# The values of a windowed cross attention: from 64x64 tiles in halves to 32x64 tiles by blocks of 32 keys

## What is computed

```python
qh, kh = rope(q @ wq.T), rope(k @ wk.T)             # 16 heads of 64
vh = v @ wv.T
scores = einsum('bhqd,bhkd->bhqk', qh, kh) * 64 ** -0.5
window_mask = (j <= i) & (j >= i - 32)              # i: query, j: key
probs = softmax(where(window_mask, scores, -1e30))
out = einsum('bhqk,bhkd->bhqd', probs, vh)          # then out @ wo.T
```

## Time and profile before

| what | value |
|---|---|
| device time, median of 3 runs | 756.9 us (753.03 to 758.53) |
| span of the profiled execution | 754.4 us |
| other time given for the profiled execution | none |
| mean granted clock of TensorE | 0.972 |
| TensorE busy (matmuls) | 712.6 us, 94% |
| VectorE / ScalarE / GpSimd busy | 540.6 / 533.2 / 530.1 us |

### The profile page before, as it was taken

One profiled execution on the slowest core, in us unless ns is written; L12 is line 12 of the kernel. 1 busy time (PEld: TensorE's weight loads), 2 busy tenths in 40 slices (PEclk: granted clock), 3 DMA queues, 4 the chain that ended last, 5 costly groups with the idle time before them and its releaser, 6 DMA issues. The chain is left out here.

```text
span 754.4 us, 31316 instructions
## 1 busy us (share of the span) xinstructions
PE 712.6 (94%) x11673; PEld 592.2 (79%) x11673; DVE 540.6 (72%) x1406; ACT 533.2 (71%) x1943; POOL 530.1 (70%) x875
## 2 busy tenths in 40 slices
PE   6889999999999999999999999999999998699990
PEld 4577788888888888888888888888888887577560
DVE  2466777777777777777787888778777776457660
ACT  2267777877777777888887877777778777555550
POOL 3266676777777877888777777777777777456554
PEclk7799999999999999999999999999999999899995
DMA  6000000211111000000000000000000000241420
GB/s 239 4 18 9 10 10 13 69 38 38 38 39 38 17 18 26 24 25 24 25 25 24 24 25 25 25 24 25 25 32 10 11 10 10 58 127 55 128 63 16
DMA packets 22802, 27.61 MB, mean 37 GB/s; under 512 B 3448, under 2 KB 18684, under 8 KB 22656
## 3 DMA queue, kind: packets, MB, share of 16 engines
q1 hardware_dynamic: 19152, 17.80, 7.8%
q0 software_dynamic: 2784, 6.56, 2.4%
q10 hardware_dynamic: 720, 1.26, 0.5%
HBM read 16.82 MB, written 9.24 MB: 35 GB/s over the span
## 5 line engine op out<-in xcount | busy, mean ns | idle before, releaser
L1123 ACT ACTIVATE PX<-P,mx 128x128 f32<-128x128 f32 x512 | 186.0, 415 | 10.1 <-DVE mx L704 10.1
L1406 POOL TENSOR_TENSOR PX<-PX,mx 128x512 f32<-128x512 f32 x128 | 130.6, 1040 | 13.5 <-DVE mx L709 13.3
L1123 ACT ACTIVATION_READ_ACCUMULATOR PX<-P,mx 128x1 f32 x512 | 130.6, 255 | 0.0
L643 DVE TENSOR_REDUCE nmf<-P 128x4 f32<-128x512 f32 x128 | 79.4, 682 | 17.5 <-PE P L226 17.5
L704 DVE TENSOR_REDUCE mx<-P 128x4 f32<-128x512 f32 x128 | 82.9, 669 | 2.6 <-PE P L326 2.6
L1132 ACT ACTIVATE PT<-P 128x512 f32<-128x512 f32 x128 | 69.7, 599 | 20.3 <-PE P L339 20.3
L1401 POOL TENSOR_TENSOR rq<-rq,tq 128x1024 f32<-128x1024 f32 x32 | 75.8, 2369 | 2.9 <-DVE tq L668 2.9
L1396 POOL TENSOR_TENSOR rk<-rk,tk 128x1024 f32<-128x1024 f32 x32 | 75.9, 2372 | 0.0
L1366 POOL CAST nm<-nmf 128x16 bf16<-128x16 f32 x32 | 6.4, 199 | 98.0 <-DVE nmf L643 98.0
L291 PE MATMUL P<-wvT,cxT 128*128 128x512 f32 x128 | 70.8, 635 | 0.4 <-ACT nmT L1080 0.4
L1087 ACT ACTIVATE PS<-P 128x512 f32<-128x512 f32 x128 | 66.5, 614 | 3.8 <-PE P L247 3.7
(11 more groups left out here) (179 smaller groups left out, 1831.4 us busy)
## 6 DMA issues: line engine op xcount, KB each, us to landing
ew<-in_ew SPq DMA_DIRECT2D x9, 384.0 KB, 3.7
xrow<-z_xs SPq DMA_DIRECT2D x24, 136.0 KB, 2.1
z_xs<-c SPq DMA_DIRECT2D x16, 136.0 KB, 3.0
x<-in_x SPq DMA_DIRECT2D x32, 64.0 KB, 2.0
cxT<-in_ctxT SPq DMA_DIRECT2D x31, 64.0 KB, 1.8
wk<-z_xs SPq DMA_DIRECT2D x6, 136.0 KB, 2.1
wvT<-z_xs SPq DMA_DIRECT2D x6, 136.0 KB, 2.1
tab<-in_tab SPq DMA_DIRECT2D x1, 512.0 KB, 7.5
```

Of the source, the lines that this page charges most:

```text
L643: dve.tensor_reduce(nmf[b % 2][:, 0, r, :], v3(bank(f"s{r}")), AX.X, ALU.max, negate=True).then_inc(S["v_bm"][r], 1)
L1123: t = act.activation(PX[(4 * b + r) % 6][:, c, :], p[:, c * 128:c * 128 + 128], ACT.Exp, bias=m[:, 0, r, c:c + 1], scale=1.0, accum_out=m[ ...
L1406: pool.tensor_tensor(X[:, :, :], X[:, :, :], mx[b % 3][:, 2, r, :].rearrange("p (h a) -> p h a", a=1).to_broadcast([128, 4, 128]), ALU.mul ...
```

## The change

The values are computed per block of 32 keys: for each head four matmuls, block r (32 rows of V, 32 of PT) with the 64 queries that see it (32 for r = 3), each block into a bank of its own (pv0 to pv3), the even and the odd head in the two halves of the output's partitions. That is eight 32x64 tiles. All 16 heads of a batch stay in the four banks, and one signal `t_pv` comes at the end of both halves. pv0 and pv2 together cover every query once, pv1 and pv3 the queries that see a second block. ScalarE copies pv2 and pv0 (512 columns each) into oX, VectorE adds pv3 (256 columns) and pv1 (512 columns) onto it. The banks are 2, 4, 5 and 6 in place of 5, 0, 2 and 4; the waits of `c_v`, `d_pt` and `d_wo` follow the merged signals. The calls of `d_pv(b, 0)` and `d_pv(b, 1)` in the written order become one `d_pv(b)` in the same place.

```diff
-            def d_pv(b, k):
-                lo = take(f"lo{k}", b, (S["s_ox"][k], b + 1))
-                hi = take(f"hi{k}", b, (S["v_ox"][k], b + 1))
-                pe.wait_ge(S[f"s_v{k}"], b + 1)
-                for u in range(2):
-                    pe.wait_ge(S["s_pt"][2 * k + u], b + 1)
-                for q in range(4):
+            def d_pv(b):
+                p = [take("pv0", b, (S["s_ox"], 2 * b + 2)), take("pv1", b, (S["v_ox"], 2 * b + 2)),
+                     take("pv2", b, (S["s_ox"], 2 * b + 1)), take("pv3", b, (S["v_ox"], 2 * b + 1))]
+                for k in range(2):
+                    pe.wait_ge(S[f"s_v{k}"], b + 1)
                     for u in range(2):
-                        pe.matmul(lo[64 * u:64 * u + 64, 96 * q:96 * q + 96], V[b % 3][0:64, 8 * k + 2 * q + u, :],
-                                  PT[(2 * b + k) % 3][0:64, 2 * q + u, 0:96], start=True, stop=True)
-                    for u in range(2):
-                        t = pe.matmul(hi[64 * u:64 * u + 64, 64 * q:64 * q + 64], V[b % 3][64:128, 8 * k + 2 * q + u, :],
-                                      PT[(2 * b + k) % 3][64:128, 2 * q + u, 64:128], start=True, stop=True)
-                t.then_inc(S["t_pv"][k], 1)
+                        pe.wait_ge(S["s_pt"][2 * k + u], b + 1)
+                    for q in range(4):
+                        for u in range(2):
+                            for r in range(4):
+                                n, h = 64 if r < 3 else 32, 2 * q + u
+                                t = pe.matmul(p[r][64 * u:64 * u + 64, n * (4 * k + q):n * (4 * k + q) + n],
+                                              V[b % 3][32 * r:32 * r + 32, 8 * k + h, :],
+                                              PT[(2 * b + k) % 3][32 * r:32 * r + 32, h, 32 * r:32 * r + n],
+                                              start=True, stop=True)
+                t.then_inc(S["t_pv"], 1)
...
-            def d_ox(b, k):
-                o, hi = oX[2 * (b % 2) + k][:, :, 64:96], bank(f"hi{k}")[:, 0:256]
-                dve.wait_ge(S["s_ox"][k], b + 1)
-                dve.tensor_tensor(o, hi.rearrange("p (h q) -> p h q", h=4)[:, :, 0:32], o, ALU.add).then_inc(S["v_ox"][k], 1)
+            def d_ox(b, i):
+                o, n = oX[b % 2], 32 if i == 0 else 64
+                o = o[:, :, 96:128] if i == 0 else o[:, :, 32:96]
+                p = bank("pv3" if i == 0 else "pv1")[:, 0:8 * n].rearrange("p (h q) -> p h q", h=8)
+                dve.wait_ge(S["s_ox"], 2 * b + 1 + i)
+                dve.tensor_tensor(o, p, o, ALU.add).then_inc(S["v_ox"], 1)
...
-            def d_ox(b, k):
-                act.wait_ge(S["t_pv"][k], b + 1)
+            def d_ox(b, i):
+                act.wait_ge(S["t_pv"], b + 1)
                 if b >= 2:
                     act.wait_ge(S["t_wo"], b - 1)
-                lo, hi = bank(f"lo{k}")[:, 0:384], bank(f"hi{k}")[:, 0:256]
-                act.activation(oX[2 * (b % 2) + k][:, :, 96:128], hi.rearrange("p (h q) -> p h q", h=4)[:, :, 32:64],
-                               ACT.Copy)
-                act.activation(oX[2 * (b % 2) + k][:, :, 0:96], lo.rearrange("p (h q) -> p h q", h=4),
-                               ACT.Copy).then_inc(S["s_ox"][k], 1)
+                o = oX[b % 2]
+                o = o[:, :, 64:128] if i == 0 else o[:, :, 0:64]
+                act.activation(o, bank("pv2" if i == 0 else "pv0").rearrange("p (h q) -> p h q", h=8),
+                               ACT.Copy).then_inc(S["s_ox"], 1)
```

More of the change, by code:

```diff
@@ L38 @@
 BANKS = dict(xt=1, xg=3, xr=2, xy=2)
-BANK = dict(a=0, cnt=2, dn=4, ds0=6, ds1=4, ds2=7, ds3=5, dt0=5, dt1=0, dt2=2, dt3=7, et=3, gu=2, hi0=0, hi1=4, kE=0,
-            kO=1, ln=1, lo0=5, lo1=2, nmt=3, oT=5, po=3, pos=4, qE=3, qO=6, qkv=1, rt=7, s0=2, s1=3, s2=0, s3=1,
+BANK = dict(a=0, cnt=2, dn=4, ds0=6, ds1=4, ds2=7, ds3=5, dt0=5, dt1=0, dt2=2, dt3=7, et=3, gu=2, pv0=2, pv1=4, pv2=5, pv3=6, kE=0,
+            kO=1, ln=1, nmt=3, oT=5, po=3, pos=4, qE=3, qO=6, qkv=1, rt=7, s0=2, s1=3, s2=0, s3=1,
             st0=1, st1=7, st2=4, st3=5, v0=7, v1=3, wo=0, x1=2, xg0=1, xg1=6, xg2=7, xg3=6, xgt0=1, xgt1=2, xgt2=3,
@@ L54 @@
 t_kE t_kO t_qE t_qO v_k1 v_k3 v_q1 v_q3 p_k p_q
-t_ds t_wo v_y v_evar p_er s_er t_et s_eT t_gu v_lg v_oh p_acc s_th v_h t_dn v_fy
+t_ds t_wo t_pv s_ox v_ox v_y v_evar p_er s_er t_et s_eT t_gu v_lg v_oh p_acc s_th v_h t_dn v_fy
 t_pos v_pse p_pos
 v_cnt v_ex v_over t_xt s_xt t_xg s_xth v_xh t_xh s_xh t_xy v_xy"""
-SETS = dict(v_bm=4, v_dm=4, s_ex=4, v_ri=4, p_pn=4, t_dt=2, s_pt=4, t_pv=2, s_ox=2, v_ox=2, s_ps=4,
+SETS = dict(v_bm=4, v_dm=4, s_ex=4, v_ri=4, p_pn=4, t_dt=2, s_pt=4, s_ps=4,
             d_x=3, d_cx=4, d_sc=4, d_xr=12, d_out=4)
@@ L124, in build @@
         PT = ring("PT", 3, [128, 8, 128])
-        oX = ring("oX", 4, [128, 4, 128])
+        oX = ring("oX", 2, [128, 8, 128])
         x2 = ring("x2_", 4, [128, 128])
@@ L363, in d_wo @@
                     pe.wait_ge(S["d_wo"], 16)
[L364 to L368, removed]
+                pe.wait_ge(S["v_ox"], 2 * b + 2)
+                for q in range(8):
+                    t = pe.matmul(p[:, 0:128], oX[b % 2][:, q, :], woT[:, q, :], start=(q == 0), stop=(q == 7))
                 t.then_inc(S["t_wo"], 1)
@@ L494, in _ @@
             first(b_pv, 2)
-            first(d_pv, 0, 0)
-            first(d_pv, 0, 1)
+            first(d_pv, 0)
             first(c_v, 3, 0)
@@ L516, in _ @@
             first(b_pv, 3)
-            first(d_pv, 1, 0)
-            first(d_pv, 1, 1)
+            first(d_pv, 1)
             first(c_v, 4, 0)
@@ L540, in _ @@
             first(b_pv, 4)
-            first(d_pv, 2, 0)
-            first(d_pv, 2, 1)
+            first(d_pv, 2)
             first(c_v, 5, 0)
@@ L581, in _ @@
                 tile(x_hT, "xr", s - 36, 0)
-                batch(d_pv, s - 5, 0)
-                batch(d_pv, s - 5, 1)
+                batch(d_pv, s - 5)
                 batch(c_v, s - 2, 0)
@@ L1111, in c_v @@
                 if b >= 3:
-                    act.wait_ge(S["t_pv"][half], b - 2)
+                    act.wait_ge(S["t_pv"], b - 2)
                 act.activation(V[b % 3][:, 8 * half:8 * half + 8, :].rearrange("p h d -> p (h d)"),
@@ L1130, in d_pt @@
                 if n >= 0:
-                    act.wait_ge(S["t_pv"][n % 2], n // 2 + 1)
+                    act.wait_ge(S["t_pv"], n // 2 + 1)
                 act.activation(PT[(2 * b + k) % 3][:, :, 64 * u:64 * u + 64],
                                bank(f"dt{r}").rearrange("p (h q) -> p h q", h=8), ACT.Copy).then_inc(S["s_pt"][r], 1)
-            def d_ox(b, k):
-                act.wait_ge(S["t_pv"][k], b + 1)
+            def d_ox(b, i):
+                act.wait_ge(S["t_pv"], b + 1)
                 if b >= 2:
                     act.wait_ge(S["t_wo"], b - 1)
-                lo, hi = bank(f"lo{k}")[:, 0:384], bank(f"hi{k}")[:, 0:256]
-                act.activation(oX[2 * (b % 2) + k][:, :, 96:128], hi.rearrange("p (h q) -> p h q", h=4)[:, :, 32:64],
-                               ACT.Copy)
-                act.activation(oX[2 * (b % 2) + k][:, :, 0:96], lo.rearrange("p (h q) -> p h q", h=4),
-                               ACT.Copy).then_inc(S["s_ox"][k], 1)
+                o = oX[b % 2]
+                o = o[:, :, 64:128] if i == 0 else o[:, :, 0:64]
+                act.activation(o, bank("pv2" if i == 0 else "pv0").rearrange("p (h q) -> p h q", h=8),
+                               ACT.Copy).then_inc(S["s_ox"], 1)
             def e_eT(b):
```

## The result

The kernel with the change takes 783.7 us (median of 4 runs, 782.14 to 785.31), the kernel before beside it on the same chip 757.7 us (753.03 to 758.86): ratio 1.0346, 95% interval 1.0315 to 1.0377, slower. The forecast was 754.5 us in a range of 746 to 766. The profiled execution has a span of 781.6 us against 754.4, so 27.2 us are to be found. TensorE is busy for about the same share of it as before, with 2048 matmul passes more.

What follows compares the result with a forecast made beforehand. The prediction took TensorE's order of work to bound the kernel: 28 batches x 0.08 us gained make 2.2 us, so the span falls from 754.4 to 752.2 and the median from 756.9 to 754.7, rounded to 754.5; range 746 to 766.

Steps and rivals of the forecast that it cites:

- The start of the block: Value block's start: waits for ScalarE's last copy of turned probabilities (bank 2), so some 0.03 us later, at 314.47.
- The block after: Value block in eight tiles: 16 passes per tile at 0.059 us plus 0.15, with 0.03 added: 1.12 us, 0.35 less.
- The bounds 1.09 and 1.94: Value block's length: at least 1.09 us by 64-column passes, at most 1.94 us at 14 ns for each of 128 passes.
- What comes due next: Copies, adds, reciprocal and product behind the block: line 318 waits 0.18 us, leaving 0.14 of 0.32 us gained.
- each 0.01 us that the block is longer is lost one to one: Chain from block to line 318: it hangs on the block's end, so extra block length is lost in full.
- 0.08 us per batch times 28, the first three and the last counted at 0: Whole kernel: 0.08 us gained in each of 28 batches, 2.2 us in all; none in the first three and the last.
- the reserve of 0.06: Per-batch gain: 0.06 us set against it because no row showed eight tiles, leaving 0.08 us.
- the 90 us behind 664.2: End of the kernel: said to hold no cross attention values and to stay as it is.
- bank 6: Start of the value block: bank 6 (the rotated queries) was said to be free about 1 us earlier.
- Eight tiles aren't fed fast enough: Rival at the value block: passes come at 14 ns, block 1.94 us, 19 us longer in all, 776 us; chance 0.19.
- The adds don't hold TensorE: Rival at line 318: the adds cause no wait, the full 0.32 us per batch stays, 747.9 us; chance 0.14.

Runs made afterwards that it cites:

- the run with 64 passes: Kernel after with blocks of 64 keys: four 64x64 tiles, 64 passes of 64 columns, its banks, signal and copies kept, adds as maxima; 755.8 us, ratio 0.997.

## Why the prediction was wrong, step by step

- *The start of the block* (some 0.03 us later): right, 0.05 us behind the last copy against 0.02.
- *"The block after"*, 1.12 us: this step failed. It took the length of a pass in one tile, 59 ns, as the limit, and the issue of eight starts at 6.7 ns each, from a burst of four at line 318, as just hidden under it. Sustained, a pass with its weight load takes 10.6 ns on the mean: 128 x 0.0106 + 0.15 = 1.51 us. A short burst doesn't measure a rate. The bounds 1.09 and 1.94 did hold the true value, and the single value was chosen from the row with four starts, not from a group with many.
- *A term that no step had*: the code itself. Eight tiles double the instructions of the densest stretch, and the next 256 are used up in less than the 2.2 to 2.8 us in which a piece becomes usable. In the block it costs 0.47 us per period, 11.8 us in all, and behind the block up to 2.9 more: together more than the slow issue. The rival had a price for the block's length only, and the block's mean of 2.01 us came out near its upper bound for this other reason. The cause rests on the traces (a load before each hole, no semaphore in sight, and each hole at the end of 256 instructions) and on the experiments with fewer or less dense instructions (0.03 and 0.07 us of holes with 64 passes, 0.13 with a pause between, 0.50 with 128 narrow ones). No run moved the ends of the pieces by themselves.
- *"What comes due next"*: right in each term. Copies 595 ns, adds 0.43 and 0.69 us, the product's end 2.49 us behind the end of the block (forecast 318.08 - 315.59 = 2.49), line 318 another 0.15 later. With a block of 1.09 us line 318 stands at +3.75; the prediction's terms with that block give 318.23 - 0.03 - 314.47 = 3.73. That "each 0.01 us that the block is longer is lost one to one" holds too: 1.51 against 1.09 us moves line 318 from +3.75 to +4.15.
- *0.08 us per batch times 28, the first three and the last counted at 0.* With the block as forecast 0.19 us per batch are gained, more than 0.08: the block is 0.03 shorter than forecast, and the reserve of 0.06 wasn't needed. But the last batches are not 0. The prediction took the 90 us behind 664.2 to hold no values; the last batch's block stands there, at 664.28. In the run with 64 passes the start of the block is 6.4 us ahead of the kernel before in batches 28 and 29, and only 0.7 us are left at the end of the span. In the last batch, the chain that ended last shows how the merged block loses there. Kernel before, four tiles, and after:

```profile
662.20 0.71 PE P L339 x16
...
664.28 0.28 PE P L353 x2
```

```profile
656.27 0.72 PE P L339 x16
...
658.27 0.50 ACT PT L1130
658.77 1.49 issue
660.26 1.16 PE P L356 x64
```

```profile
683.19 0.73 PE P L339 x16
...
685.20 0.50 ACT PT L1130
685.70 1.49 issue
687.18 1.79 PE P L356 x82
```

  From the turning (line 339) to the block it is 2.08 us before, and 3.99 us in both others. The first half could start on two copies, and the merged block needs all: its last copy ends some 2.5 us behind the start of the turning, which is about 0.4 of the 1.9 us. The other 1.49 us are called issue, but they are a wait for a bank. The block now takes bank 6, which in the last batches a tile of the routed experts holds (`xg1` and `xg3` in the table `BANK`), until VectorE's line 878 has read it. In the kernel after:

```profile
686.45 0.42 DVE L878 SCALAR_TENSOR_TENSOR xth<-xth,P 128x256 f32<-128x256 f32 x1
```

  That ends at 686.87, its semaphore comes at 686.88, and the sequencer's wait, begun at 684.48, ends 0.04 behind it; the run with 64 passes shows the same at 659.95 and 659.96. So what the prediction says of bank 6, that it is free about 1 us earlier, holds for the regular batches and not for the last one. This is 1.9 of the 5.7 us that are lost there in the run with 64 passes, and of the 7.5 after. Where the rest goes in the last 100 us is not settled; from 688.2 on the kernel after also has 3.4 us at a granted clock of 0.50 that the kernel before doesn't have there.
- *The rivals.* "Eight tiles aren't fed fast enough" was the case that came (chance 0.19), and its threshold was right: "over 1% once the block lasts about 1.5 us". Its 776 us missed the measured 783.7 by 8. "The adds don't hold TensorE" is refuted: with one add shortened line 318 comes 0.19 us earlier. The Trainium skill (TensorE: Matmul & The Clock Gate, Part 1) says that start-to-start never drops below about 25 ns. This case's traces differ: 10.6 ns on the mean over 128 passes.

Even the ideal version of the change, the block at 1.09 us, is worth 0.3%: of the 0.38 us by which it is shorter than before, the chain over the copies takes half, and the last batches take most of what is left. No variant beats the kernel before with the whole computation.

## What to carry to other kernels

Before splitting matmuls into more and smaller tiles, count instructions, not columns: total passes times the sustained rate of issue (here 10.6 ns with a weight load each) against passes per tile times the length of one, and take the larger. Then count how fast the densest 256 instructions of the engine are used up; in less than the 2.2 to 2.8 us measured here the code may come too late, in a stretch that shows no wait but "issue". To tell such a hole from others, count the engine's instructions: here the holes stand 256 or a multiple of it apart. And where two half-blocks become one, or move to other banks, work out the first and last batches too: what could start on half of its inputs now waits for all, and a bank that is free in the regular batches may be held there.

## What was not expected of the hardware

- TensorE issues weight load and pass in 10.6 ns on the mean when eight tiles take turns, in both orders tried, and nearly whatever the columns (1.44 us for 32 against 1.51 for 64).
- Within one tile an fp32 pass with its weight load of 64 columns took 58 ns, with 32 and 48 columns streamed as with 64.
- TensorE stops for up to 2.05 us in a block of 256 instructions that waits for no data, and resumes 2.2 to 2.8 us behind the start of a 16 KB load of code, each time at an instruction whose number has the same remainder (193) by 256.
- A change between 32-row and 64-row tiles costs about 0.21 us by the estimate above, with 0.15 us between the starts on its two sides: 96 passes with 15 changes take longer (4.28 us) than 128 passes without (1.51).
- The granted clock can fall in the middle of a busy kernel: to 0.50 (1.2 GHz) for 3.4 us behind a hole of 1.8 us (second add shortened) and of 2.1 us (32 columns), and in nearly every period of the run with changes of tile size; behind a hole of 2.05 us in the kernel after it stayed at 1.00.
